# Moving one copy on ScalarE ahead of one exponential in a float32 attention kernel

## The reference

```
xn = (x - moving_mean) * rsqrt(moving_var + 0.001) * gamma + beta
q = xn @ Wq + bq;  k = xn @ Wk + bk;  v = xn @ Wv + bv
scores = (q @ k.T) * 64 ** -0.5        # 128 x 128 for each row
attn = softmax(scores, axis=-1)
out = xn + (attn @ v) @ Wo + bo
```

## Time and profile before

| what | value |
|---|---|
| median of 3 runs | 5043.77 us (5042.2 to 5046.18) |
| profiled execution | 5046.96 us, of which the span is 5045.0 us |
| granted TensorE clock in it | 0.999 |
| DMA | 806.24 MB, mean 160 GB/s; 79.7% of 16 engines' span |
| first and last copy of a first half (L333) | at 51.4 and 5031.9 us |

### The profile page before, as it was taken

The page is one execution under the profiler, slowest core; times in us unless marked ns, Lnnn a source line. Parts: engine busy times, 40 slices in busy tenths (PEclk is TensorE's granted clock), DMA queues, the critical chain, the costliest instruction groups (busy, mean ns, idle before and its releaser), DMA issues.

```text
span 5045.0 us, 171155 instructions
## 1 busy us (share of the span) xinstructions
PE 4926.9 (98%) x51224; PEld 3965.0 (79%) x51224; DVE 4401.3 (87%) x6946; ACT 4320.2 (86%) x18948; POOL 4520.9 (90%) x2824
## 2 busy tenths in 40 slices
PE   7999999999999999999999999999999999999999
PEld 5777777777777777777777777777777777777777
DVE  6888888888888888888888888888888888888887
ACT  6888888888888888888888888888888888888887
POOL 6999899999999899989898999999898989898987
PEclk9999999999999999999999999999999999999999
DMA  6888888888888888888888888888888888888886
GB/s 130 162 161 162 161 162 161 161 161 161 161 161 161 162 162 162 162 161 161 161 162 162 162 161 161 161 161 162 161 161 162 162 162 162 161 161 161 162 161 126
DMA packets 4294233, 806.24 MB, mean 160 GB/s; under 512 B 4294208, under 2 KB 4294208, under 8 KB 4294208
## 3 DMA queue, kind: packets, MB, share of 16 engines
q1 hardware_dynamic: 4294208, 805.93, 79.7%
HBM read 537.10 MB, written 268.44 MB: 160 GB/s over the span
## 4 chain that ended last, share of the span: by engine, by line
PE 52%; ACT 38%; issue 9%; DVE 0%; SPq 0%; ACTq 0%; DMA 0%; DVEq 0%
ACT probs L318 27%; PE score_ps L590 20%; PE probsT_ps L625 12%; PE u_ps L609 10%; PE uo_ps L609 9%; ACT g L345 6%; ACT probsT L333 5%; PE uo_ps L648 0%; PE g_ps L635 0%; ACTq L344 0%; DMA bias_col<-in_L_conv_bv 0%; DVE attn L434 0%; PE u_ps L571 0%; DVE row_stat L468 0%; SPq L191 0%
## 5 line engine op out<-in xcount | busy, mean ns | idle before, releaser
L318 ACT ACTIVATE probs<-score_ps,neg_top 128x128 f32<-128x128 f32 x8192 | 2939.9, 394 | 652.8 <-DVE neg_top L478 652.7
L265 POOL TENSOR_TENSOR x_weighted<-x_in,row_weights 128x1024 f32<-128x1024 f32 x1024 | 2401.2, 2368 | 32.0 <-DMA x_in<-in_x 32.0
L318 ACT ACTIVATION_READ_ACCUMULATOR probs<-score_ps,neg_top 128x1 f32 x8192 | 1913.3, 234 | 0.0
L625 PEld LDWEIGHTS probsT_ps<-ident,probs 128*128 128x128 f32 x8192 | 900.3, 141 | 883.4 <-issue 882.8
L468 DVE TENSOR_REDUCE row_stat<-score_ps 128x8 f32<-128x1024 f32 x1024 | 1250.5, 1221 | 321.0 <-PE score_ps L590 321.0
L287 POOL TENSOR_TENSOR y<-attn,x_scaled_rows 128x512 f32<-128x512 f32 x768 | 980.9, 1277 | 486.0 <-DVE attn L434 486.0
L625 PE MATMUL probsT_ps<-ident,probs 128*128 128x128 f32 x8192 | 1286.4, 280 | 79.8 <-ACT probsT L333 14.4
L276 POOL TENSOR_TENSOR x_scaled_rows<-x_weighted,out_bias 128x512 f32<-128x512 f32 x1024 | 1199.4, 1197 | 0.0
L648 PE MATMUL uo_ps<-w_o,uT 128*128 128x128 f32 x8192 | 1083.3, 275 | 2.8 <-DVE attn L434 1.9
L635 PE MATMUL g_ps<-xT,w_g 128*128 128x512 f32 x2048 | 1052.6, 596 | 9.4 <-ACT g L345 5.9
L590 PE MATMUL score_ps<-xT,g 64*128 64x128 f32 x16384 | 1053.7, 278 | 1.0 <-ACT probs L318 1.0
(11 more groups left out here) (70 smaller groups left out, 2429.4 us busy)
## 6 DMA issues: line engine op xcount, KB each, us to landing
x_quads<-in_x SPq DMA_DIRECT2D x4096, 64.0 KB, 2.2
x_in<-in_x SPq DMA_DIRECT2D x1024, 256.0 KB, 3.2
out<-y SPq DMA_DIRECT2D x1024, 256.0 KB, 2.4
norm_row<-in_L_conv_gamma SPq DMA_DIRECT2D x1, 32.0 KB, 3.7
norm_row<-in_L_conv_beta SPq DMA_DIRECT2D x1, 32.0 KB, 3.7
norm_row<-in_L_conv_moving_mean SPq DMA_DIRECT2D x1, 32.0 KB, 4.2
norm_row<-in_L_conv_moving_var SPq DMA_DIRECT2D x1, 32.0 KB, 4.3
norm_row<-in_L_conv_bo SPq DMA_DIRECT2D x1, 32.0 KB, 4.2
```

The source lines that it names most:

```text
L265: nc.gpsimd.tensor_tensor(x_weighted[:, n % 4, :, 0:2 * C].rearrange("p s (h c) -> p s h c", h=2), x_in[:, n % 8, :, None, :].broadcast_to ...
L318: last = nc.scalar.activation(probs[:, n % 4, q, :], score_ps[n % 2][:, q // PAIRS, q % PAIRS * W:(q % PAIRS + 1) * W], ACT.Exp, bias=neg_ ...
L625: last = nc.tensor.transpose(probsT_ps[:, q * W:(q + 1) * W], probs[:, n % 4, half * HALF + q, :], ident[:])
```

## The change

One boundary in ScalarE's step is moved by one. Before, ScalarE made exponentials 0 to 4 of the second group, then the copy of half 0 of group 2t-1, then exponentials 5 to 7. Now it makes 0 to 3, then the copy, then 4 to 7.

```diff
@@ -351,9 +351,9 @@
                 exponentials(r, 2 * t, peeled, range(5, 7))
                 keep_g(r, 2 * t + 4, peeled)
                 exponentials(r, 2 * t, peeled, range(7, 8))
-                exponentials(r, 2 * t + 1, peeled, range(0, 5))
+                exponentials(r, 2 * t + 1, peeled, range(0, 4))
                 keep_probsT(r, 2 * t - 1, peeled, 0)
-                exponentials(r, 2 * t + 1, peeled, range(5, 8))
+                exponentials(r, 2 * t + 1, peeled, range(4, 8))
                 keep_probsT(r, 2 * t - 1, peeled, 1)
                 keep_g(r, 2 * t + 5, peeled)
```

## The result

| | us | |
|---|---|---|
| before | 5043.68 | median of 4 runs (5042.2 to 5046.18) |
| changed | 4914.59 | median of 4 runs (4913.45 to 4915.21) |
| ratio | 0.9743 | 95% interval 0.9726 to 0.976 |
| profiled execution, changed | 4914.05 | span 4912.1; clock 0.999 |

The change is worth 129.1 us, 2.6%. The forecast was 4901 with a range from 4866 to 4964: the sign, the mechanism and nine tenths of the size are as forecast; 142.5 us were expected.

What follows compares the result with a forecast made beforehand. A TensorE-ScalarE loop was taken as the bound, with ScalarE late to the second copy. 509 steps x 0.28 = 142.5 us off 5046.96 gave 4904.5, as a median 4901; range 4866 to 4964.

Steps and rivals of the forecast that it cites:

- What bounds the kernel: Whole step: a loop to and fro between TensorE and ScalarE, 9.74 us long, ScalarE's list holding back the second copy.
- The rival in which the engine with the highest share bounds the step: Whole step: another engine, GpSimd at 90%, is the bound and nothing arrives; 5044 us, chance 5%.
- The copy: Second group's first-half copy: starts just behind its transposes, next weight load 0.28 us earlier, step 9.46 us.
- The rival of a slower start behind the wait: Second group's copy: ScalarE starts more slowly after waiting, so only part arrives, 0.16 to 0.22 a step; chance 5%.
- the dearer wait: Second group's copy: waiting loses the 93 ns overlap of back-to-back ACTIVATEs, gain 0.19 us a step, 4947 us.
- From the execution to the median: Whole run: the median was taken 3.2 us below the profiled execution, turning 4904.5 into 4901 us.
- The last exponential as the thinnest cover: Second group's end on ScalarE: 0.14 us later, hidden before the next scores by about 0.06 to 0.1 us.
- the first of the signs of being wrong: TensorE: idle time moving to the scores' weight loads, through the last exponential, would show the prediction wrong.
- VectorE and GpSimd: VectorE's 0.29 us maximum wait just fits 0.28; GpSimd's second addition up to 0.07 late, with nothing on the loop waiting.
- Slower: Second group's copy: ScalarE stands there too long, keeping four exponentials behind; 5125 us at a 0.5 us wait, chance 4%.
- nothing: Whole step: another engine bounds it, so the move gains nothing; 5044 us, chance 5%.
- all of the slot: Second group's copy: the moved exponential's whole slot arrives, 0.32 to 0.34 us a step, 4881 to 4871 us; chance 8%.

Runs made afterwards that it cites:

- six in front: The kernel before with six exponentials of the second group, in place of five, ahead of its first-half copy; 5224.65 us, 1.035 of before.
- the fastest experiment: The changed kernel with the first-half copies of both groups cut to 64 of 128 columns of each matrix; 4812.45 us, 0.9541 of before.
- three in front: The changed kernel with three exponentials of the second group, in place of four, ahead of its first-half copy; 5058.46 us, 1.0023 of before.
- the first kernel with shorter copies: The changed kernel with only the second group's first-half copy cut to 64 of 128 columns of each matrix; 4871.69 us, 0.9658 of before.

## Why the prediction was right

- **What bounds the kernel.** Right: a loop over TensorE and ScalarE, in which ScalarE's list before the second copy was late. Shown by the shorter exponentials (4911.8) and, for the slope, by six in front (0.35 a step). The rival in which the engine with the highest share bounds the step, GpSimd at 90%, is refuted by the 2.6%: GpSimd did the same work, and its share went from 90% to 92%, and to 94% in the fastest experiment.
- **The copy.** Expected 0.63 behind its transposes' start, with 0.60 to its end and 0.11 to the weight load; measured 0.63, 0.60 and 0.12. The rival of a slower start behind the wait falls, and so does the dearer wait with its 0.19 a step and 4947 us. The weight load moved by 0.27 and not by 0.28, and the mean step by 0.26. That is the mis-sized term of the step: 509 x 0.02 = 10 of the 13.6 us that the forecast was too low. It was a difference of times read to 0.01 us, multiplied by 509.
- **From the execution to the median.** I took 3.2 us off, since the profiled execution of before was so much above its median; that of the changed kernel lies 0.5 below its own. That is the rest of the 13.6, and it is scatter between executions (4 us within the four of before) and not a part of the mechanism.
- **The last exponential as the thinnest cover.** Right as to place: it is the next thing to fail, as three in front showed. Its cover is 0.09 us: the read ends at 10.95, plus 0.11 is 11.06, and the load behind it comes at 11.15. That lies in the expected 0.06 to 0.1, but with luck, since two errors cancel. The load runs 0.11 ahead of its matmul (11.15 and 11.26) and not 0.06. And the read started where the sum has it, 1.78 behind the copy's start (8.95 to 10.73; 1.70 - 0.29 + 0.36 = 1.77 expected) but recorded 0.22 and not the 0.29 of before. The time didn't move to the scores' weight loads, the first of the signs of being wrong: their row of the view of waits has 90.3 us, against 89.6 before.
- **VectorE and GpSimd.** The wait of the maximum went to nothing in every second step, as said, and GpSimd's addition follows its bias at 8.50 without a pause; neither costs time. The wait for `neg_top` is 0.95, where 0.8 was expected; about half of the difference is `keep_g` in front of it, which records 0.72 and no longer 0.79.
- **Slower, nothing, all of the slot.** Refuted by the result; all of the slot was out of reach since the transposes end 0.10 after ScalarE is free, and with three in front and the last exponential held in place nothing more comes.
- **A chain that names one engine.** I expected to be wrong if ScalarE's share stayed at 38%. It fell to 0%, which says less than it seems: `keep_g` ends exactly when TensorE needs it and both first-half copies end later than that, as the shorter copies showed, and moving the first group's boundary by one in either direction costs 101 or 173 us.

## What to carry to other kernels

When an engine with an in-order list hands results to another, put a hand-over behind as much work as its input needs to be ready, and no more; the gain of moving it is the smaller of the work moved and the time to the input's own end, and the work that is moved behind it must have cover of its own. Read that time off a twin of the hand-over in the same step that already waits. Where nothing is to spare, the trace shows a fixed signal delay between two rows (0.11 us here), even if the waiting row has no idle time: `keep_g` was just on time so, and the load behind the moved copy was still 0.13 late. Look for such pairs on both sides of what is moved, whatever the chain of waits calls the bound.

## What the runs showed that was not expected

- What a late weight load costs isn't always its lateness. A load that doesn't wait starts 0.11 before its matmul (12.60 and 12.71 in the first kernel with shorter copies), one that waited 0.03 before it (9.67 and 9.70 in the changed kernel). So of the 0.13 by which the moved copy's load is late the matmuls lose 0.05, and the step 0.08. With three in front, the load was 0.29 late and the step lost 0.28.
- ScalarE's recorded durations grow while it works without a wait and fall back behind one: 0.36 to 0.44 for an exponential in one step of before, and the second group's copy shows 0.66 before and 0.60 after the change. As the end counts, such a row hides 0.06 us of a gain for whoever reads starts alone.
